# Gate weight put on the second up-projection's operand, two experts per operation, from the 13th of 32 units on; pair weights on 64 rows each; a new order of the work

## What is computed

```python
# layer 0: attention of one head over each image's 256 tokens
q, k, v = xf @ wq + bq, xf @ wk + bk, xf @ wv + bv
x = gamma * softmax(q @ k.T) @ v + x
# layer 1: 8-head attention without softmax, causal by tril
s = ln(t)                                   # over the 64 channels
Omega = (s Q_h) s^T * tril;  t = t + sum_h Omega (s E_h^T)
# mixture of 16 experts, hidden 128, all experts computed, top 2 weighted
s2 = ln(t)
probs = softmax(s2 @ gate_w + gate_b); dispatch = top 2 of probs, renormalised
hidden_e = silu(s2 @ w1_e) * (s2 @ w2_e)
t = t + sum_e dispatch[:, e] * (hidden_e @ w3_e)
```

## Time and profile before

| | before |
|---|---|
| median of 3 runs | 104.0 us (103.03 to 105.31) |
| the profiled execution's own time | 104.42 us |
| its span in the profile | 102.7 us |
| TensorE busy | 92.6 us, 90% |
| VectorE busy | 71.0 us, 69% |
| ScalarE busy | 52.8 us, 51% |
| GpSimd busy | 45.3 us, 44% |
| mean granted clock of TensorE | 0.983 |

### The profile page before, as it was taken

The page is one execution under the profiler, slowest core; times in us unless marked ns, Lnnn a source line. Parts: engine busy times, 40 slices in busy tenths (PEclk is TensorE's granted clock), DMA queues, the critical chain, the costliest instruction groups (busy, mean ns, idle before and its releaser), DMA issues.

```text
span 102.7 us, 2617 instructions
## 1 busy us (share of the span) xinstructions
PE 92.6 (90%) x954; PEld 50.9 (50%) x954; DVE 71.0 (69%) x218; ACT 52.8 (51%) x110; POOL 45.3 (44%) x57
## 2 busy tenths in 40 slices
PE   5977796999999999999992999979999999999990
PEld 4567685767758557765220353223333233333590
DVE  1347999797844929935899937999666877574451
ACT  0564978735366690657763145971445744451400
POOL 5868002211200410000459690871949699959100
PEclk9999999999999999999999589999999999999999
DMA  1569994000000000000799940000199990001002
GB/s 26 87 108 207 187 171 73 0 0 0 6 0 0 6 3 0 6 0 13 182 421 437 402 195 3 3 0 6 65 316 426 437 402 10 0 0 51 6 0 51
DMA packets 9514, 11.07 MB, mean 108 GB/s; under 512 B 6014, under 2 KB 8206, under 8 KB 8734
## 3 DMA queue, kind: packets, MB, share of 16 engines
q1 hardware_dynamic: 8492, 10.66, 33.8%
q10 hardware_dynamic: 914, 0.20, 0.9%
q0 software_dynamic: 96, 0.04, 0.8%
HBM read 10.57 MB, written 0.33 MB: 106 GB/s over the span
## 4 chain that ended last, share of the span: by engine, by line
PE 70%; DVE 12%; ACT 4%; DMA 3%; issue 3%; SPq 2%; POOL 2%; POOLq 0%; DVEq 0%
PE bank L953 27%; PE bank L972 11%; PE bank L910 4%; PE bank L853 4%; PE bank L883 3%; DMA wv_in<-in_L_conv_wv 3%; PE bank L746 3%; PE bank L838 3%; DVE qk L586 2%; PE bank L738 2%; PE bank L867 2%; DVE nmax L600 2%; PE bank L927 2%; PE bank L994 2%; PE bank L1004 2%
## 5 line engine op out<-in xcount | busy, mean ns | idle before, releaser
L406 POOL TENSOR_TENSOR hid<-uu,dbc 128x512 f32<-128x512 f32 x24 | 32.3, 1376 | 12.7 <-DVE uu L677 6.0
L953 PE MATMUL bank<-s2T,w_in 64*64 64x512 f32 x256 | 31.9, 617 | 0.8 <-ACT sil L502 0.7
L502 ACT ACTIVATE sil<-bank 128x512 f32<-128x512 f32 x32 | 19.0, 597 | 17.2 <-PE bank L953 15.0
L677 DVE TENSOR_TENSOR uu<-bank,sil 128x512 f32<-128x512 f32 x32 | 21.7, 688 | 8.9 <-ACT sil L502 5.6
L397 POOL TENSOR_TENSOR rstd<-veps,neg_half 128x2 f32<-128x2 f32 x8 | 5.6, 697 | 34.8 <-DVE veps L533 34.8
L953 PEld LDWEIGHTS bank<-s2T,w_in 64*64 64x64 f32 x256 | 9.3, 137 | 18.5 <-issue 12.1
L972 PE MATMUL bank<-hid,w_in 64*64 64x512 f32 x120 | 15.0, 591 | 0.0
L972 PEld LDWEIGHTS bank<-hid,w_in 64*64 64x64 f32 x120 | 4.6, 133 | 7.7 <-issue 6.7
L626 DVE TENSOR_TENSOR omega<-bank,tri 128x256 f32<-128x256 f32 x16 | 5.7, 416 | 1.6 <-PE bank L853 1.6
L688 DVE TENSOR_TENSOR hid<-uu,dbc 128x512 f32<-128x512 f32 (+1 forms) x9 | 6.5, 732 | 0.0
L473 ACT ACTIVATE qs<-bank 128x512 f32<-128x512 f32 x8 | 4.3, 594 | 2.9 <-PE bank L838 2.8
(11 more groups left out here) (125 smaller groups left out, 133.5 us busy)
## 6 DMA issues: line engine op xcount, KB each, us to landing
dbc<-dispatch_scratch SPq DMA_DIRECT2D x6, 1024.0 KB, 8.8
dbc<-dispatch_scratch SPq DMA_DIRECT2D x4, 512.0 KB, 4.5
w_in<-in_L_ffn_w SPq DMA_DIRECT2D x3, 512.0 KB, 8.1
x_in<-in_x ACTq DMA_DIRECT2D x1, 192.0 KB, 2.6
q_in<-in_L_attn_Q SPq DMA_DIRECT2D x2, 64.0 KB, 3.6
e_in<-in_L_attn_E SPq DMA_DIRECT2D x1, 128.0 KB, 4.3
out<-x SPq DMA_DIRECT2D x1, 128.0 KB, 2.0
out<-x SPq DMA_DIRECT2D x2, 64.0 KB, 1.7
```

What stands on the lines that cost most here:

```text
L406: nc.gpsimd.tensor_tensor(hid[:, i % HID], uu[:, i % UU], dbc[:, e, :], ALU.mult).then_inc(hid_done, 1)
L502: nc.scalar.activation(sil[:, i % SIL], banks[U1_BANK[i % 2]][:], ACT.Silu).then_inc(sil_done, 1)
L677: nc.vector.tensor_tensor(uu[:, i % UU], banks[U2_BANK[i % 3]][:], sil[:, i % SIL], ALU.mult).then_inc(uu_done, 1)
L953: last = nc.tensor.matmul(banks[bank[i % len(bank)]][C * c:C * (c + 1), :], w_in[rows, HIDDEN * e + C * c:HIDDEN * e + C * (c + 1)], s2T[r ...
```

## The change

From unit 12 on the gate weight is no longer put on uu. Since u2 is linear in s2, the weight is put on the tokens that w2 multiplies: "scale" p makes scaled[p % 4] = s2T * pair_dbc[:, p], 128x512 in one GpSimd operation, for the two units of pair p at once: the rows 64 to 127 carry the weight of unit 2p's expert, the rows 0 to 63 that of unit 2p+1's. For that the units are paired anew (unit 2k is expert k, unit 2k+1 expert k+8), and w_in holds experts 8 to 15 with w1 and w2 swapped between the row halves; it is loaded in four transfers instead of two. "up" i takes s2T for u1 and, for i >= 12, scaled for u2, and waits for the scaled pair. "times" i writes hid itself for i >= 12. "weigh" is left for units 0 to 11 (VectorE: 3, 7, 11; GpSimd: the nine others). dbc is loaded for 12 units in six transfers of 2 units, and pair_dbc in four chunks of pairs 6-7, 8-9, 10-11 and 12-15, each as two transfers to 64 rows. The list has a new order throughout, and BANKS follows it. Nothing of the other steps' code changes.

```diff
-CHUNKS = (0, 2, 4, 8, 12, 16)
+WEIGHED = 12
+WEIGHED_CHUNKS = (0, 2, 4, 8, 12)
+PAIR_CHUNKS = ((6, 8), (8, 10), (10, 12), (12, 16))
+def expert_of(unit):
+    at = unit % EXPERTS
+    return at // 2 + EXPERTS // 2 * (at % 2)
 def on_dve(unit):
-    return unit % 4 == 3
+    return unit >= WEIGHED or unit in (3, 7, 11)
...
-    [("split wqk", 0), ("transpose x", 0), ("bias", 0), ("stack x", 0), ("stack x lo", 0), ("bias col", 0),
+    [("transpose x", 0), ("split wqk", 0), ("bias", 0), ("stack x", 0), ("stack x lo", 0), ("bias col", 0),
...
-IDLE_FIRST, IDLE_AFTER = 9, {('transpose x', 0): 6, ('project qk', 0): 3}
+IDLE_FIRST, IDLE_AFTER = 9, {('transpose x', 0): 6, ('transpose x', 3): 6}
...
         def wait_hid(eng, unit, piece=0):
+            if unit >= WEIGHED:
+                eng.wait_ge(uu_done, unit + 1 + piece)
+                return
...
+        def wait_scale(eng, pair):
+            half = pair // 8
+            eng.wait_ge(pair_ld[pair_chunk(pair)], 32)
+            if pair % 8 == 0 or pair == WEIGHED // 2:
+                wait_emptied(eng, "s2T", 2 * half)
+                wait_emptied(eng, "s2T", 2 * half + 1)
+            if pair - SCALED >= WEIGHED // 2:
+                eng.wait_ge(u2_filled, 2 * (pair - SCALED) + 2)
...
+                    if i == 0:
+                        for c in range(len(WEIGHED_CHUNKS) - 1):
+                            first, last = WEIGHED_CHUNKS[c] // 2, WEIGHED_CHUNKS[c + 1] // 2
+                            for k in range(last - first):
+                                src = d_scratch[0, first + k::EXPERTS // 2, :].unsqueeze(0).to_broadcast([P, 2, HALF])
+                                sp.dma_start(dbc[:, 2 * (first + k):2 * (first + k + 1), :], src).then_inc(dbc_ld[c], 16)
+                    for c, (start, stop) in enumerate(PAIR_CHUNKS):
+                        if start // 8 == i:
+                            pairs = slice(start % 8, start % 8 + stop - start)
+                            for r in range(2):
+                                src = d_scratch[i, EXPERTS // 2 * r + pairs.start:EXPERTS // 2 * r + pairs.stop, :]
+                                sp.dma_start(pair_dbc[C * (1 - r):C * (2 - r), start:stop, :].rearrange("p e t -> p (e t)"),
...
+                if name == "scale" and not scaled_on_dve(i):
+                    wait_scale(pool, i)
+                    nc.gpsimd.tensor_tensor(scaled[:, i % SCALED], s2T[:, HALF * (i // 8):HALF * (i // 8 + 1)], pair_dbc[:, i, :],
+                                            ALU.mult).then_inc(scaled_by_pool, 1)
...
+                if name == "times" and i >= WEIGHED:
+                    dve.wait_ge(u2_filled, i + 1)
+                    dve.wait_ge(sil_done, i + 1)
+                    if i >= HID:
+                        dve.wait_ge(down_done, (i - HID) // 2 + 1)
...
+                        last = nc.vector.tensor_tensor(hid[:, i % HID, cols], banks[U2_BANK[i % 3]][:, cols], sil[:, i % SIL, cols],
+                                                       ALU.mult)
...
+                    if i >= WEIGHED:
+                        wait_scaled(pe, i // 2)
                     for m, bank, full in ((0, U1_BANK, u1_filled), (1, U2_BANK, u2_filled)):
-                        rows = slice(C * m, C * (m + 1))
+                        r = (m + i) % 2
+                        rows = slice(C * r, C * (r + 1))
+                        if m == 1 and i >= WEIGHED:
+                            moving = scaled[rows, i // 2 % SCALED, :]
+                        else:
+                            moving = s2T[rows, half * HALF:(half + 1) * HALF]
```

More of the change, by code:

```diff
@@ L40, with full_chunk, pair_chunk @@
 QUARTERS = TILES * CHUNKS_OF_TILE
-SIL, UU, HID = 3, 8, 8
-CHUNKS = (0, 2, 4, 8, 12, 16)
-def chunk_of(expert):
-    return sum(expert >= start for start in CHUNKS[1:])
+SIL, UU, HID, SCALED = 3, 8, 8, 4
+WEIGHED = 12
[4 more added lines that the diff above has]
+    return at // 2 + EXPERTS // 2 * (at % 2)
+def full_chunk(unit):
+    return sum(unit >= start for start in WEIGHED_CHUNKS[1:])
+def pair_chunk(pair):
+    return [pair < stop for start, stop in PAIR_CHUNKS].index(True)
@@ L51, in on_dve, with scaled_on_dve @@
 def on_dve(unit):
[L53 removed]
+    return unit >= WEIGHED or unit in (3, 7, 11)
+def scaled_on_dve(pair):
+    return pair in ()
 SCHEDULE = (
[L59 removed]
[4 rows of a table removed]
[L64 to L107 removed]
@@ L226, in hybrid_kernel @@
         dispT = sb("dispT", [HTILES * EXPERTS, HALVES, P])
-        dbc = sb("dbc", [P, EXPERTS, HALF])
+        dbc = sb("dbc", [P, WEIGHED, HALF])
+        pair_dbc = sb("pair_dbc", [P, EXPERTS, HALF])
+        scaled = sb("scaled", [P, SCALED, HALF])
         sil = sb("sil", [P, SIL, HALF])
@@ L287, in wait_hid, with wait_scaled @@
         def wait_hid(eng, unit, piece=0):
-            before = sum(on_dve(n) for n in range(unit + 1))
+            if unit >= WEIGHED:
+                eng.wait_ge(uu_done, unit + 1 + piece)
+                return
+            by_dve = sum(on_dve(n) for n in range(unit + 1))
             if on_dve(unit):
-                eng.wait_ge(hid_by_dve, before + piece)
+                eng.wait_ge(hid_by_dve, by_dve)
             else:
-                eng.wait_ge(hid_done, unit + 1 - before)
+                eng.wait_ge(hid_done, unit + 1 - by_dve)
+        def wait_scale(eng, pair):
[6 more added lines that the diff above has]
+                eng.wait_ge(u2_filled, 2 * (pair - SCALED) + 2)
+        def wait_scaled(eng, pair):
+            by_dve = sum(scaled_on_dve(n) for n in range(WEIGHED // 2, pair + 1))
+            if scaled_on_dve(pair):
+                eng.wait_ge(scaled_by_dve, by_dve)
+            else:
+                eng.wait_ge(scaled_by_pool, pair + 1 - WEIGHED // 2 - by_dve)
         def img(b):
@@ L315, in _ @@
             sp.dma_start(e_in[:], E.rearrange("h i k -> i h k")).then_inc(ld_e, 16)
-            for m, w in enumerate((w1, w2)):
-                sp.dma_start(w_in[C * m:C * (m + 1)].rearrange("p (e h) -> p e h", e=EXPERTS),
-                             w.rearrange("e c h -> c e h")).then_inc(ld_w, 16)
+            for m in range(2):
+                for k, w in enumerate((w1, w2) if m == 0 else (w2, w1)):
+                    experts = slice(EXPERTS // 2 * m, EXPERTS // 2 * (m + 1))
+                    sp.dma_start(w_in[C * k:C * (k + 1), experts, :], w[experts].rearrange("e c h -> c e h")).then_inc(ld_w, 16)
             sp.dma_start(gate_in[:], gate_w).then_inc(ld_gate, 16)
@@ L671, in _ @@
                                             ALU.mult).then_inc(disp_ready, 1)
-                if name == "times":
+                if name == "times" and i < WEIGHED:
                     dve.wait_ge(u2_filled, i + 1)
@@ L678, in _ @@
                                             ALU.mult).then_inc(uu_done, 1)
-                if name == "weigh" and on_dve(i):
-                    half, e = divmod(i, EXPERTS)
-                    dve.wait_ge(uu_done, i + 1)
-                    dve.wait_ge(dbc_ld[half][chunk_of(e)], 16)
+                if name == "times" and i >= WEIGHED:
+                    dve.wait_ge(u2_filled, i + 1)
+                    dve.wait_ge(sil_done, i + 1)
                     if i >= HID:
@@ L971, in _ @@
                         for n in range(2):
-                            last = nc.tensor.matmul(banks[Y_BANK[r]][C * n:C * (n + 1), :], w3_in[rows, e + n, :],
+                            last = nc.tensor.matmul(banks[Y_BANK[r]][C * n:C * (n + 1), :], w3_in[rows, expert_of(2 * i + n), :],
                                                     hid[rows, (2 * i + n) % HID], start=(e == 0), stop=(e == last_pair))
```

131 lines of the change are left out of this document (68 added, 63 removed), and 13 rows, old and new, of tables (BANKS, SCHEDULE).

## The result

The changed kernel takes 105.73 us (median of 4 runs, 105.48 to 106.04), the kernel before 104.66 us beside it (4 runs, 103.03 to 105.65). The ratio is 1.022, 95% interval 1.012 to 1.031: about 2% slower where 4% faster was forecast, and outside the range. The profiled execution took 105.48 us around a span of 103.8 us. Executions of one kernel fall in a faster and a slower group: medians and ranges here are of all runs, ratios and intervals of the faster group alone.

A forecast was written before the change was run, and what follows sets the result against it. GpSimd and VectorE bound the kernel up to 21.3 us, then TensorE and its losses between matmuls. Gains of 0.4 (first unit sooner) and 3.5 (gaps closed) made 3.9 us: 104.0 - 3.9 = 100.1 us, range 98.4 to 102.6.

The forecast's parts named there:

- the sentence on the transfers: Half 0's weight broadcasts: 3 MB in about 7.5 us from 50; half the rate still serves units 8 to 11 at 65.
- part 3: New order of the first units: TensorE's losses fall from 5.3 to 1.8 us, 3.5 gained, bounds 1.3 to 5.3.
- the sum: TensorE's waits behind the first unit: 0.7 + 0.4 + 0.2 + 0.3 = 1.6, taken as 1.8 us, in place of 5.3.
- Part 1: Less weighing: 7 us off GpSimd, worth about nothing alone; swapped row halves taken as free, at most 0.6 us in all.
- Part 2: Order up to the experts: first unit 0.4 us sooner, at 47.3; bounds 0.6 later to 1.2 sooner.
- the early gap: "normalise 2" of images 2 and 3 runs from 50.2 to 51.4, without GpSimd; transposes through at 52.1 instead of 57.4.
- Unit 8 waits 0.7, unit 9 0.4: TensorE waits 0.7 us for silu 6 behind an exp, then 0.4 for "times" 6 behind "gate top".
- "down" 4 waits 0.3: GpSimd finishes "weigh" 9 at 67.2, behind "scale" 6 and 7, while TensorE wants "down" 4 at 66.9.
- Unit 16 with 1.3 us to spare: Unit 16, wanted at 71.6, needs "scale" 8 with half 1's weights, ready at 70.3: no wait.
- The gaps move: Rival: waits at units 8, 9 and "down" 4 grow or lower the clock; 1.3 us gained, 102.7 us; chance 0.17.
- Weights ahead of the unit: Rival: half 1's pair weights ("scale" 12 to 15, unit 24) arrive too late; up to 117 us; chance 0.04.

The follow-up runs named there:

- The order alone: Kernel before with the changed kernel's order, BANKS and idle matmuls, all 32 units still weighed and transfers as before: 101.93 us, 0.982 of before.
- the best version: Changed kernel with half 0's weights stored in unit order (contiguous), six transfers, and "weigh" 9 on VectorE: 101.26 us, 0.976; in five rounds 102.04 us, 0.975.
- the run with 20 KB: Changed kernel with the two experts of a pair 20 KB apart in the scratch instead of 16, stored in two DMAs: 105.98 us (one run).
- the run with the old order and late weights: Kernel before, own order, half 0's weights in eight transfers of two experts 16 KB apart, pieces of 2 KB: 102.36 us, 0.989.
- the source mended: Changed kernel with half 0's weights stored in unit order, so contiguous; six transfers: 102.79 us with 4 KB pieces, 102.83 us with 2 KB pieces.
- the run with 2 KB pieces: Changed kernel, half 0's weights contiguous in unit order, six transfers, 64 bytes free behind each unit in SBUF so pieces stay 2 KB: 102.83 us, 0.988.

## Why the prediction was wrong

The step that failed is the sentence on the transfers in part 3: "3 MB go first, in pieces of 2 KB ... so about 7.5 us from 50 on, and half the rate would still bring units 8 to 11 their weights at 65". Two things were wrong in it.

- *The rate.* The piece size, which it worried about, costs nothing that can be measured (104.86 against 104.46 us for the kernel before). The distance of 16 KB between the two rows of a transfer, which it didn't look at, brought 125 and 217 GB/s in the windows where a contiguous source had 214 and 356, and six issues took SyncE 5.92 us in place of 3.37.
- *The check.* It asked only when the last units want their weights. The last transfer, issued at 52.64, took 12.6 us and landed at 65.2, just as the sentence allows. But "weigh" 2 and "weigh" 4 are wanted far sooner: the forecast had three weighings done by 56.3 and "down" 1 behind them. In the trace GpSimd's third began at 57.11 and its fourth at 61.78. Slow transfers are not harmless there: with the semaphore that units 4 to 7 share they cost the waits ahead of "down" 1 and 2, 4.9 us. In all TensorE lost 7.1 us up to "down" 4 where the sum had 1.8.

Point by point:

- *Part 1* (less weighing worth nothing by itself, swapped row halves free): right so far as tested. Pairs of units still take 1.72 us. The order alone gave 101.93 us, order and scaling with a contiguous source 102.8, the intervals overlapping, and so does that of the best version. That the scaling gains anything over the order alone is not shown.
- *Part 2* (first unit at 47.3): 47.15. Right in this profile; with the same order the profiles of the other versions begin it anywhere from 46.5 to 49.2, and at 50.4 in the run with 20 KB, so that 0.1 us of agreement is partly luck.
- *Part 3, the early gap*: the four operations on `s` from 50.2 in about 1.3 us; they start at 49.58 and take 1.11. Transposes forecast through at 52.1, they start at 50.83. No low clock in this profile. Right, and the reason, GpSimd kept off, is shown by the run with the old order and late weights.
- *Unit 8 waits 0.7, unit 9 0.4*: in after hidden behind the weights' wait; with the source mended 0.67, ended by silu, and in the run with 2 KB pieces 0.32 for unit 9. The two table loads and the exp took 2.87 us (55.17 to 58.04), as the 2.9 of before, not two times the 2.66 of the Trainium skill's page "ScalarE: Activation LUTs", section "What ACT_TABLE_LOAD costs": the measurement decides.
- *"down" 4 waits 0.3*: mis-sized. 0.99 in after, 1.51 and 0.80 with the source mended. "scale" 6 waits 1.04 to 1.95 us for pair weights that the walk had taken as there.
- *Unit 16 with 1.3 us to spare*: no matmul of after waits for `scaled`, nor of the versions with a contiguous source and 64-row transfers. Right.
- *The sum.* With the source mended the brackets of the 2 KB run add up to 0.67 + 0.32 + 0.80 = 1.8 us, by luck the 1.8 of the forecast, which was counted from start to start:

```profile
59.88 1.09 PE L1034 MATMUL bank<-s2T,w_in 64*64 64x512 f32 x8 [0.67 <-ACT sil L558]
61.29 1.09 PE L1034 MATMUL bank<-s2T,w_in 64*64 64x512 f32 x8 [0.32 <-DVE uu L739]
...
69.10 1.09 PE L1052 MATMUL bank<-hid,w_in 64*64 64x512 f32 x8 [0.80 <-POOL hid L458]
```

From start to start unit 8, unit 9 and "down" 4 come 0.85, 0.55 and 1.0 us late, 2.4 in place of the 0.7 + 0.4 + 0.3 of the forecast, and smaller stops ahead of the transposes, the gate and "down" 3 bring the loss from the first unit (48.34) to "down" 4 to 20.76 - 17.4 = 3.4. So the three waits were mis-sized by 1.0 us together. Of the 2.4 us between this run's span (101.2) and the forecast's (98.8), 1.0 lies ahead of the first unit (48.34 against 47.3) and 1.3 behind it (50.4 against 49.1), where these losses are.
- *The rivals.* "The gaps move" came nearest in kind: the early gain was given back whole and more, but by transfers, a cause that it didn't have; its 102.7 us was 3 short. "Weights ahead of the unit" had the right suspect, the transfers, but put it at half 1's pair weights, where no matmul waited.
